# Spreading the weight transforms over nine of ten places, in another group order, with the fold operands loaded in two steps

## The chip, the cores and the metric

One core of one Trainium2 chip runs the whole program in one launch. The metric is the device time of an execution in microseconds, the median of several. Engines are named as the profile names them: PE (TensorE, matrix products), PEld (its weight loads), DVE (VectorE), ACT (ScalarE), POOL (GpSimd) and SP (SyncE, which here only issues DMAs; SPq is its queue).

## The reference

The input is 2048 tokens of width 512. Four blocks follow, each `x = x + f(layernorm(x))`:

```python
# 1: a selective scan, 16 states n per channel
x_dbl = x @ W_xproj.T                        # -> delta_raw, B, C
delta = softplus(delta_raw @ W_dt.T + b_dt)
h_t = exp(delta * A[n]) * h_(t-1) + delta * x * B[n];  y_t = sum_n h_t * C[n]
# 2: gated feed-forward with Walsh-Hadamard transforms around both products
x = fwht(x * SU_ug) / 64
x = silu(x @ W_gate.T * s) * (x @ W_up.T * s)   # 2048 inner channels
x = (fwht(x * SU_dp) / 64) @ W_down.T * s
# 3: mixer
x, z = split(h @ W_in.T);  x = x @ conv_w.T;  out = (x * D * silu(z)) @ W_out.T
# 4: mixture of 64 experts, the 8 best of each token, 128 places each
```

## The kernel before, in words

**Chunks, states, places.** The tokens are cut into four chunks of 512 (`NCH`). Each engine has its own program, and all are written along one line of "places": `state_at(c, n, m)` = 5 + 64c + 4n + m is place m (0 to 3) of scan state n (0 to 15) of chunk c. Below, (n,m) is such a place of chunk 0, so (0,0) is place 5 and (13,0) is place 57. A state on DVE (`states`, line 1316) is `bx` (u times the broadcast B row, line 1323), four scans (line 1332), and `hc` (times the broadcast C row, line 1350); POOL then adds `hc` into y (`add`, line 1518). PE makes the two broadcast rows in two banks (`bcast_b`, line 678, for the next state, and `bcast_c`, line 686), and `bcast_c` of a state waits until `hc` of the one before is done. `hc` waits for the POOL `add` of the state before the last. ACT makes the decays (line 975). Around these, `side(pos)` does on each engine what a table puts at that place.

**Work beside the scan of chunk 0.** The Hadamard transforms of block 2 are moved into the weights. Twelve groups of four parts each (48 parts) do that: eight groups "u" (512 columns of gate or up weights) and four groups "d" (128 columns of down weights). The string `kinds` (line 278) gives their order, `prep_places` (line 280) the place of each part, one part per place. One part is 4 products on PE, which the trace counts as 8 instructions (`prep`, line 638, products at line 648), a rounded copy on ACT (`prep_hi`, lines 906 and 909), the remainder on DVE (`prep_lo`, lines 1209 and 1214; at the next place), and on SP two stores of 256 KB (`store_prep`, line 380; two places later). A "u" group has four staging slots, one for each part. A "d" group has two, so its third part waits on ACT until the first part's two stores have landed. After the last part of a group SP loads the raw weights of the group two further on (u), or of the next group (d), 1 MB.

**Butterflies.** The raw "d" weights first go through three steps on POOL (`butterfly(g, part)`, line 1532): a scaling (line 1538, one instruction) and two butterflies (line 1548, two instructions each). The table `butterflies` (line 1592) says at which place of chunk 0 each is written; in `states` of POOL (line 1570) a place does, in this order, `plain_lo`, the norms, at (9,3) and (10,3) two `correction`s of the softplus of the next chunk (lines 1561 and 1563), and the butterfly. After place 3 of a state comes `add`. The products of a "d" group wait for its last butterfly.

**Plain splits.** Sixteen blocks of other weights (`praw`) are only split: `plain_hi` on ACT and `plain_lo` on POOL (line 1554), every third place from place 7 on.

**Folds.** The mixer's `conv_w` and the x half of `W_in` are multiplied into one weight: eight `fold`s (line 652), four with columns 0 to 511 of `conv` in chunk 0, four with the other half in chunk 1, at the places of `fold_at` (line 282). A fold is 8 products (16 instructions in the trace, line 660). Its operands `winx` (2 MB) and `conv` (2 MB in each half) lie in the memory of the transform's buffers: `winx` in that of `raw_d`, blocks 0 and 1 of the eight of `conv` in that of `wsdp` and `had`, and blocks 2 to 7 in memory that nothing uses at that time. SP loads both in `prep` (line 447) after it has stored the last part of the last group, which is a "d".

**Order on SP.** SP walks along the same places: transforms, plain stores, fold stores, and at (14,0) it waits for all transform stores and loads the six buffers of `ring`, which hold the first weights of chunk 1.

Of the kernel before, what the change touches and what calls it, by code (L numbers as in the profile page):

```python
# [13 lines left out]
P = 128  # L14
# [3 lines left out]
KT = D // P  # L18
# [6 lines left out]
M1 = I1 // P  # L25
# [29 lines left out]
def build(nc, a):  # L55
# [47 lines left out]
    with top:  # L103
# [20 lines left out]
        with A:  # L124
# [43 lines left out]
            with ExitStack() as fold_only:  # L168
                winx = sb(fold_only, "winx", [P, M1, 512])
                conv = sb(fold_only, "conv", [P, M1, 512])  # L170
# [49 lines left out]
            S_wx = sem("winx_in"); S_cv = sem("conv_in"); S_pr = [sem(f"plain_in{i}") for i in range(4)]  # L220
# [54 lines left out]
            for place in range(TAIL, TAIL + RING):  # L275
                del quanta_at[place]

            kinds = [w for w in "uduuuduuduud"]
            group_of = [kinds[:i].count(kinds[i]) for i in range(len(kinds))]
            prep_places = list(range(3, 3 + 4 * len(kinds)))  # L280
            prep_at = {place: (i // 4, i % 4) for i, place in enumerate(prep_places)}
            fold_at = {state_at(0, 13, 1) + 3 * m: (0, m) for m in range(KT)} | {state_at(1, 1, 0) + 2 * m: (1, m) for m in range(KT)}
            FOLDS, PLAINS = 2 * KT, 2 * M1
            plain_at = {state_at(0, 0, 2) + 3 * i: i for i in range(PLAINS)}

# [58 lines left out]
            with nc.Block() as block:  # L344
# [17 lines left out]
                def _(sp):  # L362
# [48 lines left out]
                        src = winzT[:, i % KT, 512 * (i // KT):512 * (i // KT) + 512] if i < M1 else woT[:, i - M1, :]  # L411
                        sp.dma_start(praw[:, i % 4, :], src).then_inc(S_pr[i % 4], 16)

                    def load_conv(half):
                        sp.dma_start(conv[:, :, :], convT[:, :, 512 * half:512 * half + 512]).then_inc(S_cv, 16)

                    def fill_slots(e, n):
                        sp.dma_start(a["slots"][ds(e * P, n * P), :].rearrange("(e p) c -> p e c", p=P),
# [28 lines left out]
                    def prep(pos):  # L447
                        if pos - 2 in prep_at:
                            i, m = prep_at[pos - 2]
                            store_prep(i, m)  # L450
                            g = group_of[i] + (2 if kinds[i] == "u" else 1)
                            if m == 3 and g < kinds.count(kinds[i]):
                                sp.wait_ge(S_pmm, 4 * i + 4)
                                load_raw(kinds[i], g)
                            if (i, m) == (len(kinds) - 1, 3):
                                sp.wait_ge(S_pmm, 4 * len(kinds))
                                load_conv(0)
                                sp.dma_start(winx[:, :, :], a["winx"].rearrange("(k p) h -> p k h", p=P)).then_inc(S_wx, 16)
                        if pos - 2 in fold_at:
                            half, m = fold_at[pos - 2]  # L460
                            sp.wait_ge(S_fl, KT * half + m + 1)
                            store_mixer(PLAINS + KT * half + m)
                            if half == 0 and m == KT - 1:
                                load_conv(1)

                    def refill(pos):
                        for q in quanta_at.get(pos, ()):
# [32 lines left out]

                    for pos in range(LAST):
                        prep(pos)
                        plain(pos)
                        x3_out(pos)
                        refill(pos)
                        if pos == state_at(0, 14, 0):
                            for s in S_su:
                                sp.wait_ge(s, 16 * 16)
                            for s in S_sd:
                                sp.wait_ge(s, 16 * 16)  # L510
                            for q in range(RING):
                                load_ring(q)
                        if state_at(1, 8, 0) <= pos < state_at(3, 0, 0) and (pos - state_at(1, 8, 0)) % 6 == 0:
                            n = (pos - state_at(1, 8, 0)) // 6
                            if n < E // 4:
                                fill_slots(4 * n, 4)
                        if pos == state_at(3, 0, 0):
                            for c in range(NCH):
                                zero_rows(c)
                        if pos == DRAIN + 4:  # L520
                            sp.wait_ge(S_ya, NS * NCH)
                            for dst, src in ((gate[:, :, :], a["gateT"].rearrange("(k p) e -> p k e", p=P)), (before_f[:, :], a["before"]),
                                             (first_slot[:, :], a["first_slot"]), (number[:, :], a["number"])):
                                sp.dma_start(dst, src).then_inc(S_sm, 16)
                        if pos == TAIL + TT + 3:
                            sp.wait_ge(S_de, TT * len(HALVES))
                            sp.dma_start(chunk(acc[0], NCH - 1), xall[:, NCH - 1]).then_inc(S_x3, 16)
                        if pos == DRAIN + 16:
                            sp.wait_ge(S_yT, TT * NCH)
                            sp.wait_ge(S_sc, KT * NS * NCH)  # L530
                        for i in range(SLOTS):
                            if pos == DRAIN + 16 + 8 * i:
                                load_weights(i, i)
                        if pos == TURN + 14:
                            sp.wait_ge(n3.tp, TT * NCH)
                            for j in range(HELD):
                                sp.dma_start(held[:, j, :].bitcast(fp32), a["w_all"][3 * tile_of(len(HALVES) - 1, j) + 2]).then_inc(S_held, 16)
                            load_weights(4, 4)
                        if pos == TAIL - 6:
                            sp.wait_ge(n4.xn, 2 * TT + 2)  # L540
                            sp.wait_ge(S_x3, 16 * 3)
                            load_weights(5, 5)
                        if pos == TAIL - 1:
                            sp.wait_ge(n4.xn, 3 * TT)
                            load_weights(6, 6)
                        if pos == TAIL + 2:
                            load_weights(7, 7)
# [16 lines left out]
                def _(pe):  # L564
# [86 lines left out]

                    def fold(half, m):
                        pe.wait_ge(S_wx, 16)
                        pe.wait_ge(S_cv, 16 * (half + 1))
                        if half == 0:
                            pe.wait_ge(S_pl, 4 * (len(kinds) - 1) + m + 1)
                        else:
                            pe.wait_ge(S_fl, m + 1)
                        for k in range(M1):
                            last = nc.tensor.matmul(PF[m][:, :], winx[:, k, m * P:(m + 1) * P], conv[:, k, :],  # L660
                                                    start=(k == 0), stop=(k == M1 - 1))
                        last.then_inc(S_fm, 1)
# [848 lines left out]
                def _(pool):  # L1511
# [58 lines left out]
                    def states(c):  # L1570
                        for n in range(NS):
                            for m in range(4):
# [15 lines left out]
                                if c == 0 and (n, m) in butterflies:  # L1588
                                    butterfly(*butterflies[n, m])
                            add(c, n)  # L1590

                    butterflies = {(2, 1): (1, 0), (3, 1): (1, 1), (4, 1): (1, 2), (6, 1): (2, 0), (6, 3): (2, 1), (7, 1): (2, 2),
                                   (9, 0): (3, 0), (9, 1): (3, 1), (10, 0): (3, 2)}

                    def rows_out(i, k):
                        if (i, k) == (0, 0):
# [111 lines left out]
```

## Time and profile before

| | |
|---|---|
| median of 3 executions | 1720.03 us (1706.4 to 1729.1) |
| the profiled execution's own time | 1721.55 us |
| its span, first to last instruction | 1719.8 us |
| mean granted clock of TensorE | 0.944 |
| busy PE / DVE / POOL / ACT | 1505.3 / 1050.1 / 784.5 / 587.1 us |

A busy time is the sum over an engine's instructions; it says nothing of whether the engine set the pace. For this change the stretch of chunk 0 matters, and in it the order in time of four engines.

### The profile page before, as it was taken

The page shows a single profiled execution, that of the slowest core. Times are in us where ns is not written, and L with a number is a line of the kernel's source. Part 1 is how long each engine was busy: PE and PEld are TensorE (multiplying, and loading weights), DVE is VectorE, ACT ScalarE, POOL GpSimd, SP SyncE. Part 2 cuts the span into 40 slices and gives each one's busy share as a digit, 9 for nine tenths or more (in the row PEclk, how much of TensorE's full clock was granted, in tenths as well). Part 3 has the DMA queues.
Part 4 walks back from the last instruction along what each step waited for, and adds up shares of the span by engine and source line. Part 5 has one row for each costly group of instructions (what it writes and reads, how often), then busy time and mean ns, then how long its engine had stood idle before and what let it go on. Part 6 is the DMA issues. An engine that isn't in the chain of part 4 may idle for free. (4 is left out here: it accounts for less than half of the span.)

```text
span 1719.8 us, 18840 instructions
## 1 busy us (share of the span) xinstructions
PE 1505.3 (88%) x5792; PEld 1037.8 (60%) x5792; DVE 1050.1 (61%) x1535; ACT 587.1 (34%) x1050; POOL 784.5 (46%) x483
## 2 busy tenths in 40 slices
PE   6999966899948899988999999999984799998992
PEld 2444423577736777766787778888863455555551
DVE  4887688887889887888988854552443122222220
ACT  4444633344534346343333322121210222222220
POOL 3467853343744444644545425763257223222232
PEclk8999988999979999999999999999996899999996
DMA  6899663356654667657565557997760799999986
GB/s 205 253 285 281 195 221 134 98 158 191 201 155 138 214 204 225 206 171 258 166 188 167 176 168 278 377 357 237 249 201 26 222 324 324 321 319 307 307 218 126
DMA packets 193539, 380.39 MB, mean 221 GB/s; under 512 B 20994, under 2 KB 95106, under 8 KB 192944
## 3 DMA queue, kind: packets, MB, share of 16 engines
q1 hardware_dynamic: 165360, 322.89, 59.4%
q0 software_dynamic: 20032, 39.92, 9.7%
q10 hardware_dynamic: 8064, 16.55, 2.8%
q8 instruction: 42, 0.69, 0.2%
q14 instruction: 41, 0.34, 0.1%
HBM read 301.65 MB, written 124.35 MB: 248 GB/s over the span
## 5 line engine op out<-in xcount | busy, mean ns | idle before, releaser
L1518 POOL TENSOR_TENSOR y<-y,hc 128x2048 f32<-128x2048 f32 x64 | 293.1, 4579 | 250.3 <-DVE hc L1350 250.3
L598 PE MATMUL bank<-tokT,ring 128*128 128x512 f32 x768 | 308.7, 402 | 12.4 <-DVE xall L1202 7.1
L1332 DVE TENSOR_TENSOR_SCAN bx<-bank,state,bx 128x512 f32<-128x512 f32 x256 | 312.5, 1265 | 0.8
L600 PE MATMUL bank<-tokT,ring 128*128 128x512 f32 x768 | 303.1, 395 | 0.0
L599 PE MATMUL bank<-tokT,ring 128*128 128x512 f32 x768 | 302.6, 394 | 0.0
L975 ACT ACTIVATE bank<-dl,an 128x512 f32<-128x512 f32 x256 | 171.0, 684 | 332.3 <-DVE bx L1332 332.2
L1524 POOL TENSOR_TENSOR act<-th,act 128x512 fp32r<-128x512 f32 x88 | 116.0, 1318 | 261.0 <-ACT act L899 260.4
L854 PE MATMUL bank<-wgu,xeT 128*128 128x384 f32 x512 | 178.2, 492 | 0.0
L598 PEld LDWEIGHTS bank<-tokT,ring 128*128 128x128 f32 x768 | 146.7, 191 | 48.6 <-issue 17.2
L610 PE MATMUL bank<-ring,act 128*128 128x512 f32 x352 | 145.2, 412 | 24.6 <-DVE th L1182 19.3
L600 PEld LDWEIGHTS bank<-tokT,ring 128*128 128x128 f32 x768 | 146.2, 190 | 32.2
L599 PEld LDWEIGHTS bank<-tokT,ring 128*128 128x128 f32 x768 | 146.6, 191 | 29.8
L1350 DVE TENSOR_TENSOR hc<-bx,bank 128x2048 f32<-128x2048 f32 x64 | 145.9, 2280 | 23.4 <-PE bank L686 22.8
L1323 DVE TENSOR_TENSOR bx<-u,bank 128x2048 f32<-128x2048 f32 x64 | 145.9, 2280 | 11.2 <-PE bank L678 8.0
L1600 POOL DMA_INDIRECT slots<-row,idx x128 | 126.8, 991 | 53.5 <-issue 41.2
L611 PE MATMUL bank<-ring,act 128*128 128x512 f32 x352 | 141.1, 401 | 0.0
L612 PE MATMUL bank<-ring,act 128*128 128x512 f32 x352 | 140.9, 400 | 0.0
L1175 DVE SCALAR_TENSOR_TENSOR th<-th,bank 128x512 f32<-128x512 f32 x96 | 65.5, 683 | 112.0 <-ACT th L894 94.5
L854 PEld LDWEIGHTS bank<-wgu,xeT 128*128 128x128 f32 x512 | 93.1, 192 | 52.9 <-issue 2.1
L1652 POOL DMA_INDIRECT acc<-ye,tok x32 | 49.3, 1541 | 164.4 <-ACT ye L1130 89.0
L871 PE MATMUL bank<-wde,hT 96*128 96x512 f32 x256 | 120.6, 593 | 0.5 <-DVE hT L1500 0.5
L648 PE MATMUL bank<-raw_u,had 128*128 128x512 f32 x256 | 115.8, 603 | 0.7 <-DMA raw_u<-wgT_in 0.7
(151 smaller groups left out, 2010.7 us busy)
## 6 DMA issues: line engine op xcount, KB each, us to landing
ring<-w_all SPq DMA_DIRECT2D x286, 512.0 KB
wgu<-wgu_in SPq DMA_DIRECT2D x64, 768.0 KB
wde<-wd_in SPq DMA_DIRECT2D x64, 384.0 KB
slots<-empty_in SPq DMA_DIRECT2D x16, 1154.0 KB, 8.4
w_all<-staged_u SPq DMA_DIRECT2D x64, 256.0 KB, 3.4
xe<-slots ACTq DMA_DIRECT2D x56, 288.5 KB
w_all<-fst SPq DMA_DIRECT2D x48, 256.0 KB, 3.9
w_all<-staged_d SPq DMA_DIRECT2D x32, 256.0 KB, 3.8
```

Of the source, the lines that this page charges most:

```text
L598: nc.tensor.matmul(b[:, :], w[:, k, 0, :], x[:, 0, k, :], start=(k == 0), stop=False)
L599: nc.tensor.matmul(b[:, :], w[:, k, 0, :], x[:, 1, k, :], start=False, stop=False)
L600: last = nc.tensor.matmul(b[:, :], w[:, k, 1, :], x[:, 0, k, :], start=False, stop=(k == KT - 1))
L610: nc.tensor.matmul(PF[t][:, :], act8[:, 0, j, tok], w[:, 0, :], start=(j == 0), stop=False)
L611: nc.tensor.matmul(PF[t][:, :], act8[:, 0, j, tok], w[:, 1, :], start=False, stop=False)
L612: last = nc.tensor.matmul(PF[t][:, :], act8[:, 1, j, tok], w[:, 0, :], start=False, stop=(j == pairs - 1))
L854: last = nc.tensor.matmul(CG[i % 2][:, 0:2 * FE], xeT[:, i % 2, k, :], wgu[i][:, k, :], start=(k == 0), stop=(k == KT - 1))
L975: nc.scalar.activation(dA[k % 2][:, :], dl[c % 2][:, k, :], ACT.Exp, scale=an[:, k, n:n + 1]).then_inc(S_dA, 1)
L1323: nc.vector.tensor_tensor(bx[:, :, :], u[:, :, :], PB[:, :].unsqueeze(1).to_broadcast([P, KT, CH]), ALU.mult).then_inc(S_bm, 1)
L1332: nc.vector.tensor_tensor_scan(bx[:, k, :], dA[k % 2][:, :], bx[:, k, :], state[:, k, n:n + 1], ALU.mult, ALU.add).then_inc(S_sc, 1)
L1350: nc.vector.tensor_tensor(hc[:, :, :], bx[:, :, :], PC[:, :].unsqueeze(1).to_broadcast([P, KT, CH]), ALU.mult).then_inc(S_cm, 1)
L1518: nc.gpsimd.tensor_tensor(y[c % 2][:, :, :], y[c % 2][:, :, :], hc[:, :, :], ALU.add).then_inc(S_ya, 1)
```

## The change

The order of the groups changes from u d u u u d u u d u u d to u d u u d u u d u u d u, so that the last group is a "u". The 48 parts no longer stand at the 48 places 3 to 50, (11,1), but at 48 of the 54 places 3 to 56, (12,3); left free are (1,2), (3,3), (6,0), (8,1), (10,2) and (12,2). The "d" groups begin at places (0,2), (4,0), (7,1) and (10,3), before at (0,2), (4,2), (7,2) and (10,2). The butterflies move with them. The four folds of chunk 0 stand at (13,2), (14,0), (14,3) and (15,1), before at (13,1), (14,0), (14,3) and (15,2). SP loads six blocks of `conv` (1.5 MB) and `winx` after the last "d" group, that is beside the last "u" group, and the two blocks that lie over `had` (0.5 MB) when the last product of the transforms is done. The six ring loads move from (14,0) to (14,3).

```diff
-            kinds = [w for w in "uduuuduuduud"]
+            kinds = [w for w in "uduuduuduudu"]
-            prep_places = list(range(3, 3 + 4 * len(kinds)))
+            prep_places = [3 + 53 * i // 47 for i in range(4 * len(kinds))]
-            fold_at = {state_at(0, 13, 1) + 3 * m: (0, m) for m in range(KT)} | {state_at(1, 1, 0) + 2 * m: (1, m) for m in range(KT)}
+            fold_at = {state_at(0, 13, 2) + 5 * m // 2: (0, m) for m in range(KT)} | {state_at(1, 1, 0) + 2 * m: (1, m) for m in range(KT)}
...
-                    def load_conv(half):
-                        sp.dma_start(conv[:, :, :], convT[:, :, 512 * half:512 * half + 512]).then_inc(S_cv, 16)
+                    def load_conv(half, blocks):
+                        sp.dma_start(conv[:, blocks, :], convT[:, blocks, 512 * half:512 * half + 512]).then_inc(S_cv, 16)
...
-                            if (i, m) == (len(kinds) - 1, 3):
+                            if (i, m) == (len(kinds) - 2, 3):
+                                sp.wait_ge(S_pmm, 4 * (len(kinds) - 1))
+                                load_conv(0, slice(2, M1))
+                                sp.dma_start(winx[:, :, :], a["winx"].rearrange("(k p) h -> p k h", p=P)).then_inc(S_wx, 16)
+                            if (i, m) == (len(kinds) - 1, 2):
                                 sp.wait_ge(S_pmm, 4 * len(kinds))
-                                load_conv(0)
-                                sp.dma_start(winx[:, :, :], a["winx"].rearrange("(k p) h -> p k h", p=P)).then_inc(S_wx, 16)
+                                load_conv(0, slice(0, 2))
...
-                                load_conv(1)
+                                load_conv(1, slice(0, M1))
...
-                        if pos == state_at(0, 14, 0):
+                        if pos == state_at(0, 14, 3):
...
-                        pe.wait_ge(S_cv, 16 * (half + 1))
+                        pe.wait_ge(S_cv, 16 * (half + 2))
...
-                    butterflies = {(2, 1): (1, 0), (3, 1): (1, 1), (4, 1): (1, 2), (6, 1): (2, 0), (6, 3): (2, 1), (7, 1): (2, 2),
-                                   (9, 0): (3, 0), (9, 1): (3, 1), (10, 0): (3, 2)}
+                    butterflies = {(2, 1): (1, 0), (2, 3): (1, 1), (3, 1): (1, 2), (6, 0): (2, 0), (6, 2): (2, 1), (7, 0): (2, 2),
+                                   (9, 1): (3, 0), (9, 3): (3, 1), (10, 1): (3, 2)}
```

## Rows read from the trace of the kernel before

**Rows 1.** Stretches: length, busy PE, PEld, DVE, ACT, POOL, PEclk, DMA share, GB/s.
```profile
44.90:279.40 234.50, 206.21 (x491) 92.21 (x489) 187.80 (x158) 110.00 (x188) 146.31 (x59) 0.95 0.80 238
279.40:527.00 247.60, 207.19 (x796) 150.38 (x796) 206.10 (x188) 102.09 (x172) 115.47 (x51) 0.90 0.50 154
...
223.00:242.00 19.00, 3.43 (x6) 1.26 (x5) 18.44 (x13) 10.36 (x14) 10.11 (x3) 0.64 0.92 310
```

**Rows 2.** PE in order of time: start, us, instructions, and [idle before, releaser].
```profile
74.32 7.03 PE L648 MATMUL bank<-raw_u,had 128*128 128x512 f32 x16
80.79 0.80 PE L678 MATMUL bank<-xdr,sel 128*128 128x512 f32 x1
...
109.60 3.70 PE L648 MATMUL bank<-raw_d,had 128*128 128x512 f32 x8 [2.32 <-POOL raw_d L1548]
...
206.96 5.40 PE L648 MATMUL bank<-raw_d,had 128*128 128x512 f32 x8 [2.75 <-POOL raw_d L1548]
...
222.78 0.80 PE L678 MATMUL bank<-xdr,sel 128*128 128x512 f32 x1
...
241.24 9.17 PE L660 MATMUL bank<-conv,winx 128*128 128x512 f32 x16 [2.84 <-DMA winx<-winx_in]
249.85 0.80 PE L678 MATMUL bank<-xdr,sel 128*128 128x512 f32 x1
250.49 7.03 PE L660 MATMUL bank<-conv,winx 128*128 128x512 f32 x16
```

**Rows 3.** DVE in order of time, columns as in rows 2.
```profile
72.86 2.27 DVE L1323 TENSOR_TENSOR bx<-u,bank 128x2048 f32<-128x2048 f32 x1
...
79.58 0.75 DVE L1209 SCALAR_TENSOR_TENSOR staged_u<-bank,vec,staged_u 128x512 fp32r<-128x512 f32 x1 [1.43 <-ACT staged_u L906]
...
86.12 2.27 DVE L1323 TENSOR_TENSOR bx<-u,bank 128x2048 f32<-128x2048 f32 x1
...
161.11 2.29 DVE L1350 TENSOR_TENSOR hc<-bx,bank 128x2048 f32<-128x2048 f32 x1 [1.14 <-PE bank L686]
...
192.08 2.28 DVE L1350 TENSOR_TENSOR hc<-bx,bank 128x2048 f32<-128x2048 f32 x1
...
228.04 2.29 DVE L1323 TENSOR_TENSOR bx<-u,bank 128x2048 f32<-128x2048 f32 x1 [0.20 <-DVE hc L1350]
...
237.75 2.29 DVE L1323 TENSOR_TENSOR bx<-u,bank 128x2048 f32<-128x2048 f32 x1 [0.20 <-DVE hc L1350]
...
279.42 2.28 DVE L1323 TENSOR_TENSOR bx<-u,bank 128x2048 f32<-128x2048 f32 x1
```

**Rows 4.** POOL in order of time, states 5 to 10.
```profile
131.48 4.54 POOL L1518 TENSOR_TENSOR y<-y,hc 128x2048 f32<-128x2048 f32 x1 [9.09 <-DVE hc L1350]
...
152.05 4.68 POOL L1548 TENSOR_TENSOR raw_d<-raw_d 128x1024 f32<-128x1024 f32 x2
...
186.71 4.69 POOL L1548 TENSOR_TENSOR raw_d<-raw_d 128x1024 f32<-128x1024 f32 x2
191.35 1.29 POOL L1554 TENSOR_TENSOR fst<-praw,fst 128x512 fp32r<-128x512 f32 x1
...
197.77 4.51 POOL L1518 TENSOR_TENSOR y<-y,hc 128x2048 f32<-128x2048 f32 x1
202.24 4.67 POOL L1548 TENSOR_TENSOR raw_d<-raw_d 128x1024 f32<-128x1024 f32 x2
```

**Rows 5.** ACT at (9,2), the copy that `plain_lo` of (9,3) waits for.
```profile
190.18 0.61 ACT L913 ACTIVATE fst<-praw 128x512 fp32r<-128x512 f32 x1
```

**Rows 6.** Issue of `winx` on SP; that of `conv` stands right before it.
```profile
227.23 0.84 SPq L458 DMA_DIRECT2D winx<-winx_in  x1
```

**Rows 7.** DMA issues of 226 to 242 us: count, KB each, us from issue to landing.
```profile
winx<-winx_in SPq DMA_DIRECT2D x1, 2048.0 KB, 14.0
w_all<-fst SPq DMA_DIRECT2D x4, 256.0 KB, 10.0
w_all<-staged_d SPq DMA_DIRECT2D x2, 256.0 KB, 3.7
```

## The prediction, made before the changed kernel was run

> **What bounds the kernel now.** I read first the table of stretches, then the order in time of PE, DVE and POOL inside chunk 0, then SP's issues and their landings. In chunk 0 PE is busy 206.2 of 234.5 us and DVE 187.8 of 234.5 [rows 1]: two engines that pass work to each other, and neither has much room. The hole is after the last transform. It ends before the broadcast at 222.78, and the first fold starts at 241.24, released by `winx` [rows 2]; in 223 to 242 us PE has 3.43 us of work at a granted clock of 0.64, while the DMA engines are 0.92 busy [rows 1]. The hole is the load of the fold operands: `conv` right before and `winx` at 227.23 [rows 6], which landed after 14.0 us [rows 7]: 227.23 + 14.0 = 241.2. What the change can win is this hole, 241.24 - 222.78 = 18.5 us less the broadcasts in it, some 16 us. It can only be won if the transforms that are put into it had not been needed earlier, that is if the steps before it run faster with nine parts where there were ten.
>
> **Part 1: fewer parts in a state.** On PE two parts take 80.79 - 74.32 = 6.47 us [rows 2], 3.23 each; a broadcast takes 0.64 to the next start (249.85 to 250.49 [rows 2]). A state with four parts is 4 x 3.23 + 2 x 0.64 = 14.2 us on PE, one with three 11.0. On DVE a state with four takes 86.12 - 72.86 = 13.26 us, of which 1.43 is a wait for ACT [rows 3]: the copy for (n,0) is queued on ACT behind the decays that wait for the second scan. A bare state takes 237.75 - 228.04 = 9.71 [rows 3], so a remainder costs (13.26 - 9.71 - 1.43)/4 = 0.53 to 0.7; a state with three parts takes 12.6 on DVE, and 11.2 if the free place is (n,0). Per pair of states PE falls from 28.4 to 25.2, but DVE only from 26.5 to 25.9. So thinning gains until DVE is the bound, 1.3 us a state at most: I take about 1 us in each of states 2 to 6. The free places also cost PE small waits, because `bcast_c` needs the last `hc`: by this count hc of state 6 ends at 142 (before at about 147.5: POOL's add of it, 4.5 us, ran up to the butterfly at 152.05 [rows 4]), with PE having done two or three parts fewer.
>
> **Part 2: the second and third d group meet POOL.** d1 begins at (4,0) in place of (4,2). By my count of POOL's queue its last butterfly ends near 98; PE arrives at 94 and waits 4 us, against 2.32 before [rows 2]. d2 begins at (7,1). From the start of the add of state 5 to the end of the last butterfly POOL needs (152.05 + 4.68) - 131.48 = 25.2 us without a gap [rows 4], and the change leaves this chain as it is; the add starts at 129.6, so d2 is ready at 154.8. PE is there at 150.0, a place earlier and less late than before, and waits 4.8 us. Then two parts and a broadcast: hc of state 7 at 154.8 + 6.5 + 0.6 = 161.9, before 161.11 [rows 3]. The lead is gone. State 8 has three parts, 12.4 us: hc at 174.3. State 9 is set by ACT (the softplus and the rounding of chunk 1 stand there ahead of the transform's copies) in both: hc at 191.8 (192.08 [rows 3]).
>
> **Part 3: the fourth d group.** Before, POOL did the first butterfly of d3 at (9,1), at 186.71, in the time before ACT's plain copy (190.18 + 0.61) let it go on at 191.35 [rows 4, 5]. Now that butterfly is at (9,3), behind that copy and behind the two corrections. The chain is 190.8 + 1.3 (plain) + 5.2 (two corrections: 197.77 less 192.6, the end of the plain) + 4.7 + 4.5 (add) + 4.7 = 211.2; before it ended at 202.24 + 4.67 = 206.9 [rows 4, 5]. d3 thus starts at about 211, one place later than before but 4 us later on the clock. PE comes at about 202 and waits 9 us. After a wait of 2.75 us the 8 instructions of a part took 5.40 us, after one of 2.32 they took 3.70 [rows 2]; I take 1.4 us more here. From 211 come eight parts (25.9) and four broadcasts (2.6) and this 1.4: the last transform ends at 240.9, before at 222.8.
>
> **Part 4: loads and folds.** SP issues `winx` and six blocks of `conv` after the remainder of the last d part, about 227.5: no earlier than before (227.23 [rows 6]). 3.5 MB at the pace of the 4 MB that took 14.0 to 14.6 us lands near 240.5. The two last blocks go out at 240.9 plus 0.6, behind one part's stores; 256 KB blocks landed in 3.7 us on a loaded queue and in 10.0 behind 4 MB [rows 7]. I take 3.7, the nearer row, and both ends for the range: first fold at 245 (241.24 before). DVE by then: `bx` of state 11 at 211.8, of 12 at 227 (three parts, and the first remainders late by PE), hc of 12 at 239.5, scans of 13 done at 249.7, its hc and the fold's remainder by 255, `bx` of state 14 at 255 (before, not ahead of its broadcast's end at 250.5). Behind it two folds, one at (15,1) in place of (15,2), so its ACT copy no longer stands behind the four copies that begin y of chunk 1. From first fold to `bx` of chunk 1 it was 279.42 - 241.24 = 38.2 [rows 2, 3]; I count 34 at full clock, 36 with the slow first fold (9.17 us for its 16 instructions, against 7.03 for those of the second [rows 2]). Half of that: 245 + 35 = 280, before 279.42: +0.6 to +1.
>
> The Trainium skill has a rule on the two-step load. "DMA: Bandwidth & Descriptors", section "Anatomy of one DMA", says that each DMA pays about 2.0 us whatever its size, plus its bytes over 436 GB/s: 0.5 MB would be 3.2 us, and the split pays the fixed part a second time, behind the last transform. By it the first fold would start at 244.7. The trace agrees roughly: 3.7 us for 256 KB [rows 7].
>
> **Part 5: after chunk 0.** The second half of `conv` is asked for some 4 us earlier against chunk 1; so I put it at nothing (without the cover of the chunk's first state it would cost half of the 14.0 us that 4 MB took [rows 7], 7). The ring loads, 3 MB, go three places later but still 17 places before their first use. From chunk 1 on the program is the same and moves as a block: PE is 207 of 247.6 us busy there [rows 1].
>
> **The sum.** Waits on PE up to the first fold, by engine order: before 2.3 + 2.75 + 1.4 + some 16 [rows 2]; now 1.3 + 4 + 3 (transposes behind `bx`) + 4.8 + 9 + 1.4 + 3. That is 22.5 and 26.5, of which the fold's later place and full clock give back some 3; the hole is not closed, it is cut into pieces. Change +1 us on the profiled 1721.55, which lies 1.5 above the median of 1720.03: 1722.5 for a like execution, 1721 for a median.
>
> The skill's "TensorE: Matmul & The Clock Gate", section "HAM oscillation", says that idle gaps drop the clock to half until activity returns. Taken strictly, the pieces at d2, d3 and the fold would each cost up to the 2.1 us of the slow fold, together +4 in place of my +2.5: 1722.5. The trace shows both sides: 0.64 in the hole [rows 1], but no slow part after the 2.3 us wait at the second d group.
>
> **The rivals.**
> (a) The hole is won. If POOL isn't the bound at d3 (butterflies quicker in place, or the corrections early), d3 starts at 202 to 207 and the last transform ends at 232 to 237. `winx`, issued before 222, lands at 236, and the fold starts at 236: 9 us gained, 1711. For it: PE's 15 idle us before 241; against it: the POOL chain, which has no gap in it [rows 4].
> (b) Slower: the last blocks of `conv` come late. They are asked for only when the last product is done, and up to 2 MB of stores of the last group and of a plain block share the queue. If they land after the 10.0 us of a queued block [rows 7] in place of 3.7, the fold starts at 251, and everything behind it moves: +6 on +1, 1728. It decides from a landing later than 244.5. For it: DMA share 0.92 in the hole [rows 1].
> (c) The change does its work but chunk 1 swallows what is lost or won (its own waits on POOL's last add set its start): 1720, inside the forecast.
>
> **How the numbers follow.** Forecast with (c), a shift of -2 to +4: 0.5. (a), -3 to -12: 0.28. (b), +5 to +12: 0.22. The likeliest gives 1721. The executions before spread over 1706.4 to 1729.1, 1.3%, so the range of the time is that of the shift, -9 to +7, with some 5 us of spread: 1709 to 1732. A measurement of this kernel tells 2% (34 us) from no change; no case reaches it, so within 2% has 0.97, faster 0.02, slower 0.01.
>
> **What would show it.** Right: products at the fourth d group released by POOL after a wait of 6 to 10 us, starting at 209 to 213; the last transform at 238 to 243; the first fold released by a DMA at 243 to 248; `bx` of chunk 1 at 278 to 283. Wrong in step 3 if d3 doesn't wait; in step 4 if the fold follows the last broadcast without a wait; in part 1 if hc of state 6 isn't ahead; and in all if chunk 1 begins before 274 or after 288.

## The result, and the profile after

The changed kernel takes 1733.32 us (median of 20 executions, 1728.74 to 1741.85), the kernel before 1726.9 (20 executions, 1706.4 to 1733.24). The ratio of the two sets is 1.0055, 95% interval 1.0036 to 1.0073: 0.55% slower, some 9.5 us (the medians alone are 6.4 us apart). The forecast was 1721 with a range of 1709 to 1732, a shift of +1. The time lies outside, on the side of rival (b). Part of that distance is the starting point: the forecast was added to a median of three executions, 1720.03, and 20 executions put the same kernel 6.9 us higher. The shift is wrong even so, since it lies beyond the +7 of the range.

The profiled execution took 1734.75 us. Its stretches, the first from the start of chunk 0 to the first `bx` of chunk 1 and the second the 247.6 us behind that, as in [rows 1] (length, busy PE, PEld, DVE, ACT, POOL, PEclk, DMA share, GB/s), and the wait for the last load:

```profile
44.90:289.40 244.50, 205.34 (x477) 90.21 (x475) 188.78 (x159) 109.72 (x188) 144.81 (x59) 0.95 0.78 232
289.40:537.00 247.60, 206.35 (x796) 150.67 (x796) 206.24 (x187) 102.50 (x173) 116.80 (x51) 0.89 0.49 151
243.30:252.30 9.00, 0.84 (x3) 0.22 (x2) 8.80 (x7) 3.32 (x6) 7.31 (x2) 0.72 1.11 365
```

Chunk 0 is 10.0 us longer (244.5 in place of 234.5 us) with the same work on every engine; the 247.6 us behind it hold nearly the same work. From the first `bx` of chunk 1 to that of chunk 2 it is 238.6 us (289.43 to 528.01), before 239.1 (279.42 to 518.47). So the loss is made in chunk 0 and carried on as a block. The span grew by 13.1 us: the first indirect add of the last stage comes 9.1 us later (1365.6 in place of 1356.5), and the other 4 arise behind it, in a stage that the change doesn't touch; no run shows why they differ between these two executions.

PE in order of time (start, us, instructions, idle before and its releaser), the rows that answer to [rows 2]; line numbers are three higher than before:

```profile
97.61 3.70 PE L651 MATMUL bank<-raw_d,had 128*128 128x512 f32 x8 [1.94 <-POOL raw_d L1551]
...
155.23 8.71 PE L651 MATMUL bank<-raw_d,had 128*128 128x512 f32 x16 [4.24 <-POOL raw_d L1551]
...
213.52 8.59 PE L651 MATMUL bank<-raw_d,had 128*128 128x512 f32 x16 [6.68 <-POOL raw_d L1551]
...
240.04 3.60 PE L651 MATMUL bank<-raw_u,had 128*128 128x512 f32 x8
244.96 0.50 PE L689 MATMUL bank<-xdr,sel 128*128 128x512 f32 x1 [1.33 <-DVE hc L1353]
252.30 9.66 PE L663 MATMUL bank<-conv,winx 128*128 128x512 f32 x16 [6.83 <-issue]
261.39 0.80 PE L681 MATMUL bank<-xdr,sel 128*128 128x512 f32 x1
```

Every d group behind the first now waits for POOL, 1.9, 4.2 and 6.7 us, and behind the two longer waits 16 instructions take 8.71 and 8.59 us in place of 7.03, at a mean granted clock of 0.82 and 0.83 (1.00 would be 2.4 GHz throughout; the lower of the two levels is 1.2 GHz). The last transform ends at 240.04 + 3.2 = 243.3. The first fold starts at 252.30, 11 us later than before, after a wait whose releaser the profile puts down as "issue". DVE in order of time, answering to [rows 3]:

```profile
164.22 2.29 DVE L1353 TENSOR_TENSOR hc<-bx,bank 128x2048 f32<-128x2048 f32 x1 [2.35 <-PE bank L689]
...
245.11 2.29 DVE L1326 TENSOR_TENSOR bx<-u,bank 128x2048 f32<-128x2048 f32 x1 [0.20 <-DVE hc L1353]
...
262.62 0.69 DVE L1224 TENSOR_TENSOR fst<-bank,fst 128x512 fp32r<-128x512 f32 x1 [7.47 <-ACT fst L916]
...
289.43 2.29 DVE L1326 TENSOR_TENSOR bx<-u,bank 128x2048 f32<-128x2048 f32 x1 [0.20 <-DVE hc L1353]
```

POOL in order of time, answering to [rows 4]: the scaling of the fourth d group, then a wait for the plain copy of ACT, the copy's remainder, and only behind the corrections (four instructions, the last one shown) the butterfly, the add and the second butterfly:

```profile
184.83 4.54 POOL L1541 TENSOR_TENSOR raw_d<-raw_d,wsdp 128x2048 f32<-128x2048 f32 x1
193.29 1.28 POOL L1557 TENSOR_TENSOR fst<-praw,fst 128x512 fp32r<-128x512 f32 x1 [3.92 <-ACT fst L916]
...
198.47 1.27 POOL L1566 TENSOR_TENSOR spr<-spr,spc 128x512 f32<-128x512 f32 x1
199.69 4.65 POOL L1551 TENSOR_TENSOR raw_d<-raw_d 128x1024 f32<-128x1024 f32 x2
204.31 4.53 POOL L1521 TENSOR_TENSOR y<-y,hc 128x2048 f32<-128x2048 f32 x1
208.79 4.67 POOL L1551 TENSOR_TENSOR raw_d<-raw_d 128x1024 f32<-128x1024 f32 x2
```

SP's queue in order of time, where `winx` answers to [rows 6], and the landings of 230 to 253 us, answering to [rows 7] (count, KB each, us from issue to landing):

```profile
232.35 0.79 SPq L458 DMA_DIRECT2D winx<-winx_in  x1
234.40 8.69 SPq L387 DMA_DIRECT2D w_all<-staged_u  x4
243.14 2.45 SPq L407 DMA_DIRECT2D w_all<-fst  x2
245.63 1.07 SPq L387 DMA_DIRECT2D w_all<-staged_u  x2
246.75 0.73 SPq L415 DMA_DIRECT2D conv<-convT_in  x1
```

```profile
winx<-winx_in SPq DMA_DIRECT2D x1, 2048.0 KB, 12.8
w_all<-staged_u SPq DMA_DIRECT2D x8, 256.0 KB, 5.7
conv<-convT_in SPq DMA_DIRECT2D x1, 1536.0 KB, 8.0
...
conv<-convT_in SPq DMA_DIRECT2D x1, 512.0 KB, 5.5
```

`winx` is there at 232.35 + 12.8 = 245.2, but the two late blocks are asked for only at 246.75 and land 5.5 us later, at 252.3, where the first fold starts. Between the last product (243.3) and their issue SP was busy with two stores of a plain block and two of a transform.

Where in chunk 0 the 10 us arise shows in the starts of `bx` (us; the last row is run 4 below, the changed kernel with three edits):

| `bx` of state | 7 | 8 | 11 | 13 | chunk 1 |
|---|---|---|---|---|---|
| before | 147.24 | 163.91 | 215.43 | 237.75 | 279.42 |
| changed | 143.36 | 167.03 | 214.39 | 245.11 | 289.43 |
| run 4 | 143.71 | 167.33 | 214.70 | 241.78 | 277.31 |

The thinner states gain 3.9 us up to state 7, and the wait at the third d group takes them back and 3.1 more. At state 11 the changed kernel is still 1.0 us ahead. States 11 and 12, which now have more parts, some of them behind (11,1) where there were none, then take 30.7 us in place of 22.3. That had to be paid back behind state 13, where the hole was; but from there to chunk 1 it takes 44.3 us, before 41.7, and only 35.5 in run 4.

### The profile page after: what moved, and what is told of

Read it like the earlier page. It is cut to its first block and busy times, and to the rows that moved or that the text cites. A ratio compares the mean times of both kernels' runs of the same rounds, so it can differ in the third digit from the quotient of the medians.

```text
span 1732.9 us, 18841 instructions
## 1 busy us (share of the span) xinstructions
PE 1500.1 (87%) x5792; PEld 1034.5 (60%) x5792; DVE 1052.3 (61%) x1535; ACT 586.6 (34%) x1050; POOL 784.7 (45%) x483
## 5 line engine op out<-in xcount | busy, mean ns | idle before, releaser
L1353 DVE TENSOR_TENSOR hc<-bx,bank 128x2048 f32<-128x2048 f32 x64 | 146.0, 2282 | 22.3 <-PE bank L689 21.6
L1655 POOL DMA_INDIRECT out<-ye,tok x32 | 49.3, 1542 | 187.8 <-ACT ye L1133 138.8
```

## The experiments

Times are medians of 10 to 12 executions (4 in runs 7 and 9, one in run 12); each ratio is against the kernel before, with its 95% interval. Since several effects are below what a ratio resolves, the start of chunk 1 (first `bx`, 279.42 before, 289.43 after, both from one profiled execution each) is read beside it. A profiled execution need not be a typical one: those of runs 4 and 11 were the fastest of their kernels (1715.77 us with a median of 1721.04, 1714.18 with 1719.7), that of run 6 was 6 us below its median (1722.83, 1728.92) and that of run 9 the slowest of four (1746.18).

**1. The butterfly of the fourth group back in its gap.**

```diff
-(9, 1): (3, 0), (9, 3): (3, 1), (10, 1): (3, 2)}
+(9, 0): (3, 0), (9, 1): (3, 1), (10, 1): (3, 2)}
```

> The changed kernel, with the scaling and the first butterfly of the fourth d group back at (9,0) and (9,1). Theory POOL (the butterfly behind the two corrections delays the group, and all behind it moves with it): products of that group start at 209 us in place of 213.5, the wait before them falls from 6.7 to about 2 us, the last transform ends near 239, first fold near 248, bx of chunk 1 near 285 in place of 289.4. Rival (the first fold is set by the DMA queue alone, which is full in that stretch anyway): the group starts at 209, but the first fold stays at 251 to 252 and bx of chunk 1 at 288 to 289.

Ratio 1.0019 (0.9998 to 1.0040), 1726.59 us. PE in order of time:

```profile
209.89 8.83 PE L651 MATMUL bank<-raw_d,had 128*128 128x512 f32 x16 [2.81 <-POOL raw_d L1551]
...
250.09 9.21 PE L663 MATMUL bank<-conv,winx 128*128 128x512 f32 x16 [7.52 <-issue]
```

The group starts 3.6 us earlier and its wait falls from 6.7 to 2.8. The last transform ends at 239.9. But the first fold comes only 2.2 us earlier, and chunk 1 begins at 286.78, 2.65 earlier, where the POOL theory said 4.4 and its rival under 1.5. So the butterfly's place costs. Part of it is hidden under the late load, which now goes out 4.7 us behind the last product (244.60) and not 3.4.

**2. The two late blocks asked for before the stores.** On SP the wait and the load move from the third to the second part of the last group:

```diff
-if (i, m) == (len(kinds) - 1, 2):
+if (i, m) == (len(kinds) - 1, 1):
```

> The changed kernel, with the load of the two last conv blocks issued one place earlier on SP, ahead of a plain store and the stores of a transform. Theory late load (the 3.4 us from the end of the last product, 243.3, to its issue at 246.75 and the stores ahead of it in the queue set the first fold): issue at 243.4 to 243.8, landing 5.5 us later at 249, bx of chunk 1 near 286 (3.4 earlier). Rival (the queue is full and drains at its own pace, so that an earlier issue only waits longer in it): landing and first fold stay at 251 to 252. Rival (winx, landed at 245, or PE's broadcast is what the fold waits for): no move at all.

Ratio 1.0025 (0.9993 to 1.0057), 1729.98 us. SP and PE in order of time:

```profile
243.52 1.39 SPq L415 DMA_DIRECT2D conv<-convT_in  x1
```

```profile
249.23 9.46 PE L663 MATMUL bank<-conv,winx 128*128 128x512 f32 x16 [3.92 <-issue]
```

Issued 3.2 us earlier, landed after 5.6 us at 249.1, fold at 249.23, chunk 1 at 286.17: 3.3 us earlier, as the late-load theory has it. The queue did not keep the gain.

**3. The late blocks used last.** The folds go through blocks 2 to 7 first; the load of blocks 0 and 1 counts on the semaphore of the raw d weights, whose four loads are done by then.

```diff
-for k in range(M1):
+for n, k in enumerate([2, 3, 4, 5, 6, 7, 0, 1]):
+    if n == 6 and half == 0:
+        pe.wait_ge(S_rawd, 16 * 5)
```

> The changed kernel, each fold of the first half going through conv blocks 2 to 7 first and waiting for blocks 0 and 1 only before its last two products. Theory late load: first fold starts when winx is there, 245.5 us, does 12 of its 16 instructions by 250.5, waits until 252.3 and ends at 254 in place of 261.4; bx of chunk 1 near 282 to 283 (7 earlier), about the time of the kernel before plus 3. Rival (the folds aren't what sets the end of chunk 0, but DVE is): the fold ends early and bx of chunk 1 moves by less than 3.

Ratio 1.0018 (0.9991 to 1.0045), 1728.09 us. PE:

```profile
247.36 5.42 PE L666 MATMUL bank<-conv,winx 128*128 128x512 f32 x12
254.38 1.98 PE L666 MATMUL bank<-conv,winx 128*128 128x512 f32 x4 [1.61 <-DMA conv<-convT_in]
```

The profile now names the load as the releaser. In this execution everything up to state 12 ran about 2 us later; chunk 1 begins at 283.85, 5.6 earlier than in the changed kernel, and 7.5 if the 2 us are taken off, as expected. The rival, DVE as what sets the end of chunk 0 at once, falls.

**4. All three edits.**

> The changed kernel with the three edits together. Theories POOL and late load both right and additive in part: last transform at 239, first fold at 242 to 243 without a wait of more than a few us, bx of chunk 1 at 276 to 278 in place of 289.4, which is 2 to 3 us ahead of the kernel before (279.4) and in time 0 to 3 us faster than it. Rival (thinning the parts to nine of ten places costs by itself): bx of chunk 1 stays at 280 or later, and the kernel isn't faster than before.

Ratio 0.9992 (0.9970 to 1.0013), 1721.04 us. First fold at 242.70 after a wait of 0.58, chunk 1 at 277.31: the three edits remove 12.1 us, the change had cost 10.0, and the result is 2 us ahead of the kernel before in the profile and level with it in time. PE's first fold:

```profile
242.70 7.13 PE L666 MATMUL bank<-conv,winx 128*128 128x512 f32 x16 [0.58 <-DMA winx<-winx_in]
```

Theories and sizes held. What remains of the change wins nothing that can be measured, so the spacing and the order were taken apart next.

**5. The kernel before, with six blocks of `conv` loaded at (9,2).** Only `winx` and two blocks are left behind the last transform.

```diff
+                        if pos == state_at(0, 9, 2):
+                            load_conv(0, slice(2, M1))
...
-                                load_conv(0)
+                                load_conv(0, slice(0, 2))
```

> The kernel before (its order, its places, its butterflies), with six of the eight conv blocks loaded at (9,2) and only winx and two blocks behind the last transform. Theory load (the hole is the time of the bytes asked for behind the last transform): 2.5 MB in place of 4, landed near 227 + 9.5 = 236.5, so the first fold starts right behind the broadcast at 237.6, at 238.3 in place of 241.2, and bx of chunk 1 at 276 to 277 (279.4 before): 3 us faster. Rival (stores and other transfers fill the queue, the bytes before the last transform cost as much there): no gain, or a later third or fourth group, bx of chunk 1 at 279 or later.

Ratio 0.9981 (0.9947 to 1.0014), 1720.4 us, not told apart from the kernel before. Chunk 1 begins at 279.61, so the forecast of the profile missed. The part behind the edit did what was expected: from `bx` of state 11 (218.70) it took 60.9 us, before 64.0 (279.42 - 215.43), and the fold stood right behind its broadcast. The 3 us were lost from state 4 to state 7, before the early load was issued: the second d group waited 3.32 us and its 8 instructions then took 6.74 us, against 2.32 and 3.70 [rows 2].

```profile
109.83 6.74 PE L650 MATMUL bank<-raw_d,had 128*128 128x512 f32 x8 [3.32 <-POOL raw_d L1550]
```

Up to there the two programs are the same, so that is a spread between executions, and a profile of one execution can't resolve 3 us here.

**6. The new order and the two-step load without the spacing.**

```diff
-prep_places = [3 + 53 * i // 47 for i in range(4 * len(kinds))]
+prep_places = list(range(3, 3 + 4 * len(kinds)))
...
+butterflies = {(2, 1): (1, 0), (2, 2): (1, 1), (3, 0): (1, 2), (5, 1): (2, 0), (5, 3): (2, 1), (6, 0): (2, 2),
+               (8, 1): (3, 0), (8, 3): (3, 1), (9, 0): (3, 2)}
```

> The changed kernel with its group order and its two-step load, but one part at every place from 3 to 50 and the folds at the places of before; the butterflies moved ahead to match. Theory spacing (nine of ten places moves the last transform from 222 to 243 us and with it the load of the last two blocks): last transform ends at 222 to 226, operands are there by 232, first fold right behind the broadcast at 237 to 239, bx of chunk 1 at 276 to 278, 12 us ahead of the changed kernel. Rival (the order of the groups costs by itself, through POOL and the two staging slots of the d groups): last transform at 230 or later, bx of chunk 1 at 283 or later.

Ratio 1.0022 (0.9992 to 1.0053), 1728.92 us. PE:

```profile
98.01 5.43 PE L651 MATMUL bank<-raw_d,had 128*128 128x512 f32 x8 [6.24 <-POOL raw_d L1551]
...
242.02 0.79 PE L689 MATMUL bank<-xdr,sel 128*128 128x512 f32 x1 [6.43 <-DVE hc L1353]
242.61 8.16 PE L663 MATMUL bank<-conv,winx 128*128 128x512 f32 x16
```

The last transform ends at 226.3, chunk 1 begins at 279.78, 9.7 us earlier than with the spacing and 2 to 4 later than expected. PE waited 6.24 us for the second d group, which is now asked for at (3,2): `bx` of state 4 was at 107.87, before at 103.34. The operands of the first fold were there at 232.69 + 5.7 = 238.4, yet it started at 242.61, behind a broadcast that waited 6.43 us for DVE's `hc`. So the fold wasn't held by a load any more, but by DVE. By the ratios, the kernel without the spacing is 0.33% ahead of the changed one; the 9.7 us come from an execution that was fast for its kernel.

**7. The spacing without the new order.** The order, the butterflies and the single load of before; parts, folds and the ring loads at the places of the change (in run 9 too).

> The kernel before with its group order and its single load behind the last transform, but the parts at the 48 places up to (12,3) and the folds at the places of the change. Theory spacing: last transform ends at 236 to 241, the 4 MB land 15 to 16 us behind it at 253 to 257, bx of chunk 1 at 288 to 292, 9 to 13 us later than before. Rival (thinning speeds the states so that the last transform comes at 225 to 230): bx of chunk 1 at 280.

Ratio 1.0193 (1.0136 to 1.0250), 1758.51 us, chunk 1 at 308.11, far beyond the forecast. One row of POOL in order of time says why:

```profile
200.62 4.53 POOL L1538 TENSOR_TENSOR raw_d<-raw_d,wsdp 128x2048 f32<-128x2048 f32 x1 [17.89 <-DMA raw_d<-wdT_in]
```

I had left the butterflies where they were, while the raw weights now come later; POOL stood 17.9 us before (9,0) and held back what it does behind that, its adds and the corrections of the softplus; ACT, which rounds the copies of the transforms, waited 8.5 us for one of these corrections. The run says little of the spacing, and was repeated as run 9.

**9. The spacing alone, butterflies moved along**, to (7,1), (7,2), (8,0) and (10,1), (10,2), (11,0).

> The spacing alone once more (order and single load of before, parts at the 48 places up to (12,3)), now with the butterflies of the third and fourth d group moved behind the later arrival of their raw weights, which POOL waited 17.9 us for in the last kernel. Theory spacing: last transform ends at 238 to 243, the 4 MB are asked for 3 to 5 us later behind stores and land 14 us after that, first fold at 257 to 260, bx of chunk 1 at 293 to 297, 1% slower than before. Rival (what made the last kernel slow was only the late butterfly, spacing costs nothing): bx of chunk 1 at 280 to 284.

Ratio 1.0108 (1.0056 to 1.0159), 1743.17 us. PE:

```profile
229.97 10.20 PE L648 MATMUL bank<-raw_d,had 128*128 128x512 f32 x16 [7.22 <-POOL raw_d L1548]
...
267.10 8.71 PE L660 MATMUL bank<-conv,winx 128*128 128x512 f32 x16 [18.17 <-DMA winx<-winx_in]
```

The last transform ends at 247.1, the fold waits 18.2 us for the load, chunk 1 begins at 303.29: 24 us later than before, more than the 14 to 18 forecast, since the third group waited 4.3 us and the fourth 7.2 as well. So these 24 us are the spacing together with the POOL steps that its later raw weights pushed back, and not the spacing by itself. In this form it costs 1.1%; with the new order and the two-step load 0.55% are left, though the two intervals overlap.

**8. Everything filled: contiguous parts, new order, all edits, folds at (12,0), (12,3), (13,2), (14,1)**, six blocks of `conv` at (8,2), butterflies as in run 6.

```diff
-fold_at = {state_at(0, 13, 2) + 5 * m // 2: (0, m) for m in range(KT)} | ...
+fold_at = {state_at(0, 12, 0) + 3 * m: (0, m) for m in range(KT)} | ...
```

> The group order of the change with one part at every place up to (11,1), six conv blocks at (8,2), winx beside the last u group, two blocks used last and asked for first, and the four folds at (12,0), (12,3), (13,2) and (14,1). Theory: nothing is waited for behind the last transform, so the hole of 16 us is filled by folds: last transform near 222 to 225, first fold at 227 to 230, bx of chunk 1 at 264 to 270, 10 to 15 us faster than the kernel before. Rival (DVE and the POOL adds set states 12 to 15, or the d groups wait): bx of chunk 1 at 275 or later, gain under 5 us.

Ratio 0.9982 (0.9952 to 1.0013), 1720.54 us. The first fold starts at 228.32, 13 us earlier than before, and chunk 1 begins at 279.29, as before: the rival was right. DVE in order of time, `bx` and `hc` of states 12 to 15 and `bx` of chunk 1:

```profile
232.97 2.29 DVE L1330 TENSOR_TENSOR bx<-u,bank 128x2048 f32<-128x2048 f32 x1 [0.20 <-DVE hc L1357]
...
242.23 2.29 DVE L1357 TENSOR_TENSOR hc<-bx,bank 128x2048 f32<-128x2048 f32 x1
244.72 2.29 DVE L1330 TENSOR_TENSOR bx<-u,bank 128x2048 f32<-128x2048 f32 x1 [0.20 <-DVE hc L1357]
...
254.62 0.68 DVE L1228 TENSOR_TENSOR fst<-bank,fst 128x512 fp32r<-128x512 f32 x1
255.22 2.28 DVE L1330 TENSOR_TENSOR bx<-u,bank 128x2048 f32<-128x2048 f32 x1
...
267.57 2.29 DVE L1330 TENSOR_TENSOR bx<-u,bank 128x2048 f32<-128x2048 f32 x1 [0.20 <-DVE hc L1357]
...
279.29 2.29 DVE L1330 TENSOR_TENSOR bx<-u,bank 128x2048 f32<-128x2048 f32 x1 [0.20 <-DVE hc L1357]
```

With no hole on PE, a state still takes 10.5 to 12.3 us: DVE's own bare 9.7 [rows 3] and what stands beside it. From `bx` of state 12 to chunk 1 it is 46.3 us, before 51.4. That is what filling the hole was worth here, 5.1 us, and the wait of 6.22 us at the second d group (`bx` of state 4 at 108.33, before at 103.34) had eaten it.

**10. The same, with the three POOL steps of each d group in a row, ahead of the add.**

```diff
+butterflies = {(2, 1): (1, 0), (2, 2): (1, 1), (2, 3): (1, 2), (5, 1): (2, 0), (5, 2): (2, 1), (5, 3): (2, 2),
+               (8, 1): (3, 0), (8, 2): (3, 1), (8, 3): (3, 2)}
```

> The kernel of the run with contiguous parts and early folds, with the three POOL steps of each d group at three places in a row of one state, ahead of that state's add ((2,1) to (2,3), (5,1) to (5,3), (8,1) to (8,3)). Theory (the 6.2 us that PE waited for the second group put all states behind it 5 us later): that wait falls under 1 us, bx of state 4 at 103 in place of 108, bx of chunk 1 at 273 to 275, 4 to 6 us faster than the kernel before. Rival (the adds, now 4.7 us later on POOL, hold up hc of the next state): bx of state 4 at 106 or later and no gain.

Ratio 0.9932 (0.9906 to 0.9959), 1710.95 us: faster than both kernels, 0.68% below the one before, the only run whose interval lies below 1. PE in order of time:

```profile
92.91 5.40 PE L652 MATMUL bank<-raw_d,had 128*128 128x512 f32 x8 [1.93 <-POOL raw_d L1555]
...
220.18 7.47 PE L667 MATMUL bank<-conv,winx 128*128 128x512 f32 x16 [1.59 <-DMA winx<-winx_in]
```

The wait at the second group is 1.93 (I had said under 1), the others are gone, `bx` of state 4 is at 104.31, and chunk 1 begins at 270.92, 8.5 us earlier than before and 2 to 4 better than expected. Behind `bx` of state 12 nothing changed: 46.3 us, as in run 8.

**11. The changed kernel with the edits of run 4 and compact steps ((6,0) to (6,2), (9,0) to (9,2)).**

> The changed kernel with the three edits of before (early butterfly, load first, blocks last) and the three POOL steps of each d group at places in a row, ahead of that state's add ((2,1) to (2,3), (6,0) to (6,2), (9,0) to (9,2)). Theory (the waits for the third and fourth d group, 4.3 and 2.8 us, and the slow clock behind each are all that spacing still costs): no wait at the third group, hc of state 7 at 158 in place of 164.5, bx of chunk 1 at 269 to 272, 7 to 10 us faster than before. Rival (state 9 and 10 are set by ACT's softplus, the adds come late): bx of chunk 1 at 275 or later.

Ratio 0.9993 (0.9966 to 1.0019), 1719.7 us. No group waits for POOL any more and hc of state 7 comes at 159.96 in place of 164.2, but chunk 1 begins at 276.08, not at 269 to 272: the last transform ends at 232.6, and the fold, at (13,2), starts only at 239.34, behind the broadcast that waits for hc of state 12. It then takes 9.26 us, where that of run 4 took 7.13.

```profile
237.77 0.79 PE L692 MATMUL bank<-xdr,sel 128*128 128x512 f32 x1 [4.82 <-DVE hc L1356]
239.34 9.26 PE L666 MATMUL bank<-conv,winx 128*128 128x512 f32 x16 [0.77 <-DMA winx<-winx_in]
```

The rival was right on the number. Of its causes, ACT shows in states 9 and 10, where DVE waits 4.8 and 5.3 us for it. At state 13 the run was 3.9 us ahead of run 4 (237.92 and 241.78), at chunk 1 only 1.2: the place of the fold and its slow products cost there, and no run separates the two.

Runs 10 and 11, which have no wait for POOL beyond the 1.93 us, are the nearest thing to a test of the spacing by itself: with it chunk 1 begins 5.2 us later, and the median is 8.8 us longer. The places of the folds and of the load of six blocks differ between them too. Between runs 8 and 4, where the butterflies stand apart, no cost of the spacing shows (279.29 without it, 277.31 with it, the times level).

**12. Run 8 with the remainders of the transforms for 64 of 512 columns** (the others are zero, so the output differs).

> The kernel with contiguous parts and early folds, where the remainder of each of the 48 transforms is computed for 64 of its 512 columns only (the others are zero). Question: what sets chunk 0 once the hole is filled. Theory lockstep (states with four parts are set by PE at 14.2 us, states without by DVE at 9.7 and more, and neither engine can run a state ahead, since the C broadcast waits for hc): 0.5 us less DVE work in each of 44 parts changes nothing that counts, bx of state 12 at 230 to 233 in place of 233.0, bx of chunk 1 at 276 to 279. Rival (DVE is the bound of the whole chunk): bx of chunk 1 at 255 to 262.

One execution, 1713.6 us. `bx` of state 12 at 227.99 in place of 232.97, chunk 1 at 275.45 in place of 279.29. That is a little more than lockstep allowed (276 to 279) and far from what a bound by DVE throughout would give (255 to 262), though DVE is busy 20 us less in chunk 0 (166.9 in place of 187.0). Of the 3.8 us, 2.6 were there at `bx` of state 1 (56.62 against 59.26). PE did not run faster for it: its C broadcasts of states 0 to 3 start 14.2 us apart in both runs. The 2.6 us went by way of POOL, whose adds and butterflies came earlier, so that the second d group started at 95.86 in place of 98.34.

## Why the prediction was wrong, point by point

**The delays were put at the right places, and the last of them was far too small.** Right or nearly so: POOL as releaser of the fourth d group with a wait of 6 to 10 us (6.68), its start at 209 to 213 (213.52, half a microsecond beyond), hc of state 7 set by the third group, hc of state 6 ahead (142.8 at its end, 142 forecast), the first fold behind a load. Wrong: that fold at 243 to 248 (252.3) and chunk 1 at 278 to 283 (289.4).

**The step that failed is in part 4, "The two last blocks go out at 240.9 plus 0.6 ... I take 3.7", the lateness of that load.** The sum had the first fold at 245; it came at 252.3. The last product ended 2.4 us later than counted (243.3), since the slow clock also struck at the third group (8.71 us for 16 instructions) and put hc of state 7 at 164.2 in place of 161.9, and with it all that followed. The issue followed 3.4 us behind it and not 0.6, because SP walks its places in order and the late load stood behind four stores, where the forecast had one part's. The landing took 5.5 us and not 3.7. That is 2.4 + 2.8 + 1.8 = 7.0 us. `winx` was forecast for 240.5 and landed at 245.2, so without the two late blocks the fold could have started at the forecast 245. Run 2 showed the second term (3.3 us back), run 3 the sum of what lies behind the last product (5.6 to 7.5 back). The last 2 us came from the first fold to chunk 1: 37.1 us and not 35, with the whole slow first fold and not half. I knew the end of the range, 10.0 us for a queued block, and priced rival (b) at +7; it was the outcome, with +9.5 to 10. Its reason was right in kind and not in size: the landing took 5.5 us and not 10.0, and it came late because it was asked for late.

The Trainium skill's formula that part 4 cites was fitted on transfers issued from POOL. It gives 2.6 us for 256 KB and 3.2 for 0.5 MB; here, on SP's queue, 3.7 [rows 7] and 5.5 were measured.

**The clock was too cheap too**, and that is inside the terms above. The slow products cost 1.7 us at the third group, 1.6 at the fourth and 2.6 in the first fold, 5.9 together; the sum had nothing, 1.4 and 1. The prediction's paragraph on the strict rule had the right number in reach: three pieces of up to 2.1 us are 6.3, and not the +4 that it writes.

**Part 3 was right in size.** The fourth d group (d3) was forecast for 211 and started at 213.5; the 2.5 us were already there at hc of state 8 (176.8, where 174.3 was forecast). Run 1 took its own delay away and moved chunk 1 by 2.65 us, a quarter of the loss.

**The first part was right about thinning, and wrong about the prize.** "What the change can win is this hole, some 16 us." A wait of PE was taken for a loss of the kernel. One row of the kernel before shows what the hole cost DVE, which sets those states:

```profile
251.08 0.69 DVE L1221 TENSOR_TENSOR fst<-bank,fst 128x512 fp32r<-128x512 f32 x1 [6.20 <-ACT fst L913]
```

Run 8 filled the hole and won 5.1 us of it. Rival (a), 9 us gained, was out of reach for the change as it stands; even the best arrangements with its spacing (runs 4 and 11) are 2 to 3 us ahead of the kernel before in the profile and level in time.

**Right:** that the spacing moves the last transform by about 20 us (222.8 to 243.3), that everything from chunk 1 on moves as a block, and that no case reaches 2%. Wrong was the chance: the slower rival had 0.22, though two of its conditions, a load issued behind the last product and a queue full of stores, stood in the diff and in [rows 7].

What the change does, in one line: parts taken out of states set by PE (14.2 us with four, which run 12 left as it was with less work on DVE) make those states a little shorter, and each part put behind them delays the one load that can't start before the last. Runs 6 and 9 give order with early load +0.4 us at chunk 1, the spacing with the old order +24, and the change has both at +10. They can't be added up, since the butterflies moved in each.

## What to carry to other kernels

A hole on one engine is worth what the engine that sets the pace waits in it: read the idle time of that engine at the same place (6.2 us here, not 16) before pricing a change that fills it. A load that must wait for the last product should be asked for ahead of all stores on its queue and used last in the sum; here these two edits, each by itself, were worth 3.3 and 5.6 to 7.5 us of a loss of 10. When a producer on an in-order engine is moved, read what stands between its old and its new place: steps put in a row ahead of the add (run 10) removed the waits that single steps behind other engines' copies had made.

## What the runs showed of the hardware that was not expected

An issue on SP can take much longer than usual while much is under way. The median issue of a store took 0.51 us in the kernel before. In the changed kernel the four behind `winx` took 8.69 us together, one pair of them 4.79 us, behind 3.5 MB that had been asked for just before (1.5 MB landed at 239.8, 2 MB at 245.2); SP waited for no engine in that time. In the kernel before, the four behind `conv` and `winx` took 6.52 us. Whether it is the bytes under way or the number of transfers that does it, no run shows.

The slow clock of PE behind a wait is not the same in each execution. Run 2 is the changed kernel up to state 12, and its second and third d groups were

```profile
98.98 5.40 PE L651 MATMUL bank<-raw_d,had 128*128 128x512 f32 x8 [2.21 <-POOL raw_d L1551]
...
156.58 7.13 PE L651 MATMUL bank<-raw_d,had 128*128 128x512 f32 x16 [2.55 <-POOL raw_d L1551]
```

In the changed kernel the same groups took 3.70 us after a wait of 1.94, and 8.71 after one of 4.24: the slow clock fell on the other group. `hc` of state 7 came at 164.0 and 164.2, so this spread evened out. In run 5 it did not: its 6.74 us, at a granted clock of 0.55, put `bx` of state 11 at 218.70 in place of 215.43. The Trainium skill says as much for the start of a kernel ("TensorE: Matmul & The Clock Gate", section "What's actually happening": the number of slow products varies from run to run); here it shows in the middle of one, at waits of 2 to 3 us.
